# Expert weights kept as f16 parts in DRAM, expert products as three f16 products, and two arrays of expert sums

## The reference

```python
x = layernorm(x + attn(x))                    # x: 16 x 56 x 256, 16 heads of 16, rope, causal window
x = layernorm(x + xattn(x, ctx))              # ctx: 16 x 1500 x 256; q and out in int8 grids
x = layernorm(x + ffn(x))                     # 8 experts, top 2 of each token

gate_probs = softmax(x @ gate_w + gate_b)
weights, selected = top_k(gate_probs, 2);  weights /= weights.sum(-1)
comb = zeros((n, E)).at[arange(n)[:, None], selected].set(weights)
h = gelu(einsum('nd,edf->enf', x, w1) + b1[:, None, :])        # d = 256, f = 1024
expert_out = einsum('enf,efd->end', h, w2) + b2[:, None, :]
out = einsum('ne,end->nd', comb, expert_out)
```

## Time and profile before

| | us |
|---|---|
| median of 3 runs | 886.67 (882.23 to 886.75) |
| the profiled execution, its own time | 884.88 |
| its span | 883.1 |

### The profile page before, as it was taken

How to read it: one execution, slowest core, us unless ns; L and a number is a source line. 1 busy time by engine, 2 the same in 40 slices (tenths; PEclk the granted TensorE clock), 3 DMA queues, 4 the chain that set the end, 5 groups by cost and what they waited for, 6 DMA issues and landing times.

```text
span 883.1 us, 30182 instructions
## 1 busy us (share of the span) xinstructions
PE 800.3 (91%) x12379; PEld 608.1 (69%) x12379; DVE 632.6 (72%) x1234; ACT 511.2 (58%) x1084; POOL 260.6 (30%) x334
## 2 busy tenths in 40 slices
PE   5689998999999989999899999999997789999996
PEld 3356766666666666666676666767665569999995
DVE  5866776768777767776777778776864736588887
ACT  2336655666566546655665665656664443687782
POOL 4233223222612251225123421522240103133332
PEclk9999999999999999999999999999999789999999
DMA  7355544554555554554555555545466855766653
GB/s 220 108 149 160 159 137 133 152 164 131 160 148 147 160 149 128 163 152 143 148 151 156 153 158 158 172 136 160 138 190 177 294 195 182 215 202 184 205 155 95
DMA packets 91377, 143.25 MB, mean 162 GB/s; under 512 B 11423, under 2 KB 79583, under 8 KB 87918
## 3 DMA queue, kind: packets, MB, share of 16 engines
q1 hardware_dynamic: 87742, 136.74, 51.8%
q0 software_dynamic: 3504, 4.62, 2.7%
HBM read 101.60 MB, written 39.68 MB: 160 GB/s over the span
## 4 chain that ended last, share of the span: by engine, by line
PE 40%; DMA 29%; DVE 10%; SPq 7%; ACT 7%; issue 5%; DVEq 0%; POOLq 0%; POOL 0%; ACTq 0%
DMA k_dram<-k_two 15%; DMA sums<-y_sb,g_token 9%; PE ps L1613 8%; PE ps L1606 7%; PE ps L1687 5%; SPq L1079 5%; PE ps L1665 4%; DMA k_st<-k_dram 4%; ACT k_two L1368 3%; DVE k_two L507 3%; PE ps L1629 3%; PE ps L1923 3%; DVE negmax L513 2%; PE ps L1944 2%; PE ps L1697 2%
## 5 line engine op out<-in xcount | busy, mean ns | idle before, releaser
L513 DVE TENSOR_REDUCE negmax<-ps 112x1 f32<-112x1500 f32 x121 | 207.3, 1713 | 44.4 <-PE ps L1629 44.1
L1395 ACT ACTIVATE pT<-ps 125x448 f32<-125x448 f32 x384 | 195.8, 546 | 18.6 <-PE ps L1665 14.7
L1230 POOL TENSOR_TENSOR ctx_lo<-ctx_raw,ctx_hi 128x250 f16<-128x250 f32 x188 | 119.3, 666 | 229.7 <-DVE ctx_hi L498 212.8
L1665 PE MATMUL ps<-qbd,k_st 97*128 97x112 f16 x1536 | 129.4, 216 | 20.2 <-ACT qbd L1351 10.8
L1665 PEld LDWEIGHTS ps<-qbd,k_st 97*128 97x128 f16 x1536 | 92.9, 99 | 78.0 <-ACT qbd L1351 27.1
L507 DVE SCALAR_TENSOR_TENSOR k_two<-ps,bk_sb,k_two 128x500 f16<-128x500 f32 x96 | 70.7, 736 | 96.7 <-ACT k_two L1368 96.7
L1368 ACT ACTIVATE k_two<-ps,bk_sb 128x500 f16<-128x500 f32 x96 | 65.1, 678 | 91.6 <-PE ps L1606 68.6
L1351 ACT COPY v_sb<-ps 125x512 f32<-125x512 f32 x96 | 56.3, 587 | 89.5 <-PE ps L1613 89.4
L1687 PE MATMUL ps<-pT,v_sb 125*17 125x56 f32 x6144 | 93.4, 217 | 10.1 <-issue 10.1
L1687 PEld LDWEIGHTS ps<-pT,v_sb 125*17 125x17 f32 x6144 | 81.5, 100 | 29.5 <-issue 19.2
L1629 PE MATMUL ps<-k_st,qbd 96*112 96x500 f16 x363 | 97.4, 375 | 3.7 <-DMA k_st<-k_dram 2.9
(11 more groups left out here) (258 smaller groups left out, 1396.0 us busy)
## 6 DMA issues: line engine op xcount, KB each, us to landing
k_st<-k_dram SPq DMA_DIRECT2D x288, 125.0 KB, 2.6
w_sb<-w SPq DMA_DIRECT2D x25, 1024.0 KB, 5.1
ctx_raw<-ctx_T SPq DMA_DIRECT2D x48, 500.0 KB, 4.5
k_dram<-k_two SPq DMA_DIRECT2D x96, 250.0 KB, 3.6
xs<-zeros SPq DMA_DIRECT2D x28, 260.0 KB, 3.1
w_sb<-w SPq DMA_DIRECT2D x8, 512.0 KB, 4.9
xg<-xs SPq DMA_DIRECT2D x21, 130.0 KB, 4.1
a_x<-x_tok SPq DMA_DIRECT2D x8, 128.0 KB, 2.8
```

The source lines that it names most:

```text
L513: V.tensor_reduce(negmax[0:QW], ps[0:QW, BANK_S:BANK_S + CHUNKS, 0:MC], AX.XY, ALU.max, negate=True).then_inc(max_done, 1)
L1230: last = nc.gpsimd.tensor_tensor(ctx_lo[:, k, c2, a], ctx_raw[:, k, c2, a], ctx_hi[:, k, c2, a], ALU.subtract)
L1395: nc.scalar.activation(pT[0:MT, (PAIRS * b + p) % 3, TPC * g:TPC * g + TPC], ps[0:MT, BANK_T + n % 2, 0:TPC * QW].rearrange("p (t n) -> p ...
L1665: last = mm(ps[:, BANK_T + n % 2, QW * i:QW * i + QW], k_st[:, j, p, a:a + P], qbd[:, j, p].rearrange("p h s -> p (h s)"), start=True, sto ...
```

## The change

- GpSimd splits the weights of all experts once, in the first stage. There are 32 pieces of 128 x 1024 elements (`PIECES`): the w2 of experts 0 to 3, all w1, the w2 of experts 4 to 7. `split_piece` multiplies a piece by W_UP = 32 in place, copies it to f16, subtracts to get the low f16 part, and stores both parts in DRAM (`w1_parts`, `w2_parts`); then it issues the load of the piece after the next. All DMAs of a piece are issued by GpSimd. Its first operation waits for the store of the piece before. Five pieces go into each `iteration`: two, one and two (`split_pieces`), until the 32 are done in the seventh.
- Both expert products are three f16 products in all 21 tiles. `load_w1` reads the parts (again 1 MB per tile), `w2_sb` holds the parts of w2. VectorE makes `xgT_hi` and `xgT_lo` in place of `xgT`, and `h_lo` in all tiles; `w2_hi` and `w2_lo` are gone. The factor 32 is taken out in the gelu's scale and in the gate.
- There are two arrays of sums in DRAM, for even and odd tiles, so an add waits only for the one two tiles before. The odd array is cleared in the batches, read back at the end, and added by four more matmuls (`carried_odd`).
- In the early tiles the second product of a tile is placed behind the first product of the next, with the routing of the last token tile between them, and VectorE's order is changed to fit. SyncE clears the spare rows after it has issued the loads of w2, not ahead of them.

```diff
+        PIECES = [(2, e, i) for e in range(E // 2) for i in range(2)] + [(1, e, i) for e in range(E) for i in range(CH)] \
+            + [(2, e, i) for e in range(E // 2, E) for i in range(2)]
...
-                V.tensor_copy(xgT[:, g % 2], ps[:, XG_BANK, 0:D].rearrange("p (c n) -> p c n", c=CH)).then_inc(xgT_done, 1)
+                src = ps[:, XG_BANK, 0:D].rearrange("p (c n) -> p c n", c=CH)
+                V.tensor_copy(xgT_hi[:, g % 2], src).then_inc(xgT_done, 1)
+                dve.wait_ge(xgT_done, 2 * g + 1)
+                V.tensor_tensor(xgT_lo[:, g % 2], src, xgT_hi[:, g % 2], ALU.subtract).then_inc(xgT_done, 1)
...
-                if g > EARLY:
-                    dve.wait_ge(added, 16 * (g - 3))
+                if g >= 4:
+                    dve.wait_ge(added[g % 2], 16 * (g // 2 - 1))
...
             for g in range(EARLY, GT):
                 if g + 1 < GT:
                     xgT_step(g + 1)
-                w2_lo_step(g)
-                if g + 1 < GT:
                     gate(g + 1)
                 if g < GT - 1:
                     h_lo_step(g)
-                    if g > EARLY:
-                        y_step(g - 1)
+                    y_step(g - 1)
...
+            sp.wait_ge(w_parts_out, 16 * len(PIECES))
             for e in range(E // 2, E):
-                sp.dma_start(w2_sb[:, e], w2[e]).then_inc(w2_in, 16)
+                sp.dma_start(w2_sb[:, e], w2_parts[e].rearrange("i p n -> p i n")).then_inc(w2_in, 16)
...
+            def load_piece(n):
+                of, e, i = PIECES[n]
+                src = w1[e, :, i] if of == 1 else w2[e, :, 4 * i:4 * i + 4].rearrange("p f n -> p (f n)")
+                nc.gpsimd.dma_start(w_raw[:, n % 2], src).then_inc(raw_in[n % 2], 16)
...
+            def split_piece(n):
+                of, e, i = PIECES[n]
+                pool.wait_ge(raw_in[n % 2], 16 * (n // 2 + 1))
+                if n > 0:
+                    pool.wait_ge(w_parts_out, 16 * n)
+                raw = w_raw[:, n % 2]
+                nc.gpsimd.tensor_scalar(raw, raw, W_UP, None, ALU.mult).then_inc(w_parts_made, 1)
+                pool.wait_ge(w_parts_made, 3 * n + 1)
+                nc.gpsimd.tensor_copy(w_hl[:, 0], raw).then_inc(w_parts_made, 1)
+                pool.wait_ge(w_parts_made, 3 * n + 2)
+                nc.gpsimd.tensor_tensor(w_hl[:, 1], raw, w_hl[:, 0], ALU.subtract).then_inc(w_parts_made, 1)
+                pool.wait_ge(w_parts_made, 3 * n + 3)
+                nc.gpsimd.dma_start((w1_parts if of == 1 else w2_parts)[e, i],
+                                    w_hl[:].rearrange("p i n -> p (i n)")).then_inc(w_parts_out, 16)
+                if n + 2 < len(PIECES):
+                    load_piece(n + 2)
...
                 ctx_lo_step(2 * it + 1, 1, 2)
+                split_pieces(it, 0, 2)
                 ctx_lo_step(2 * it + 2, 0, 0)
                 if t_before is not None:
                     b_rstd_step(t_before)
                 ctx_lo_step(2 * it + 2, 0, 1)
+                split_pieces(it, 2, 3)
                 rstd_step(it + 1)
                 ctx_lo_step(2 * it + 2, 0, 2)
+                split_pieces(it, 3, 5)
                 qbd_step(it + 1, 0, 0)
...
-                if g > 0:
-                    pool.wait_ge(added, 16 * g)
+                if g > 1:
+                    pool.wait_ge(added[g % 2], 16 * (g // 2))
...
                     f = 4 * i + q
-                    for c in range(CH):
-                        last = mm(ps[:, H_BANK + 2 * par + i, P * q:P * q + P],
-                                  w1_sb[:, par, c, P * f:P * f + P], xgT[:, par, c],
-                                  start=(c == 0), stop=(c == CH - 1))
+                    for n, (x, w) in enumerate(SPLIT):
+                        for c in range(CH):
+                            last = mm(ps[:, H_BANK + 2 * par + i, P * q:P * q + P],
+                                      w1_sb[:, par, c, F * w + P * f:F * w + P * f + P], (xgT_hi, xgT_lo)[x][:, par, c],
+                                      start=(n == 0 and c == 0), stop=(n == 2 and c == CH - 1))
...
+                pe.wait_ge(h_lo_done, g + 1)
                 for f in range(FT):
                     if g == GT - 1 and f == 4:
...
+                        pe.wait_ge(h_lo_done, g + 2)
+                    for n, (x, w) in enumerate(SPLIT):
+                        a = F * w + D * (f % 4)
+                        last = mm(ps[:, Y_BANKS[g % 2], 0:D], (h_hi, h_lo)[x][:, par, f],
...
             for g in range(EARLY, GT):
                 m1_half(g, 0)
                 if g + 1 < GT:
                     tx(g + 1)
                 m1_half(g, 1)
-                if g > EARLY:
-                    m2_split(g - 1)
-            m2_split(GT - 1)
+                m2(g - 1)
+            for q in (2, 3):
+                carried_odd(q)
+            m2(GT - 1)
```

More of the change, by code:

```diff
@@ L360, in decoder_layer @@
         row_made = sem("row_made")
-        w2_hi_done = sem("w2_hi_done")
-        w2_lo_done = sem("w2_lo_done")
+        raw_in = [sem(f"raw_in{k}") for k in range(2)]
+        w_parts_made = sem("w_parts_made")
+        w_parts_out = sem("w_parts_out")
+        odd_in = sem("odd_in")
         h_hi_done = sem("h_hi_done")
@@ L376, in decoder_layer @@
         b2_in = sem("b2_in")
-        added = sem("added")
+        added = [sem(f"added{k}") for k in range(2)]
         gate_step = sem("gate_step")
@@ L1146, in _ @@
                 keys(B - 1, 1, u)
-                for e, f in ahead[:pieces]:
-                    sp.dma_start(w2_sb[:, e, f:f + half], w2[e, :, f:f + half]).then_inc(w2_ahead, 16)
+                sp.wait_ge(w_parts_out, 16 * E)
+                for e, i in ahead[:pieces]:
+                    sp.dma_start(w2_sb[:, e, i], w2_parts[e, i]).then_inc(w2_in, 16)
                 ahead = ahead[pieces:]
@@ L1262, in qbd_step, with split_pieces @@
                     pmask[:].unsqueeze(1).unsqueeze(3).to_broadcast([KS, 4, 2, S]), ALU.mult).then_inc(qbd_done, 1)
+            def load_piece(n):
[18 more added lines that the diff above has]
+                    load_piece(n + 2)
+            def split_pieces(it, first, last):
+                for n in range(5 * it + first, min(5 * it + last, len(PIECES))):
+                    split_piece(n)
             ctx_lo_step(0, 0, 1, True)
```

182 lines of the change are left out of this document (86 added, 96 removed).

## The result

The changed kernel takes 958.41 us (median of 4 runs, 952.15 to 962.83), the kernel before in the same comparison 884.7: ratio 1.084, interval 1.079 to 1.088. I had said 888, within 866 to 910. The profiled execution took 961.3 us, its span is 959.5. Medians are of all executions of a kernel, ratios only of those within 1.5% of its fastest (the fast state). Stages are read from the one profiled execution of each kernel, and the four executions of the changed kernel lie up to 11 us apart, so a difference of a few us between the batches of two kernels is not a finding.

What follows compares the result with a forecast made beforehand. TensorE was taken to bound both the batches and the expert stage. From 884.9 us: minus 20 for expert products, plus 18 for late qbd, plus 5 for port and DMA, 887.9, left at 888; range 866 to 910.

Steps and rivals of the forecast that it cites:

- What bounds the kernel: Batches and expert stage: TensorE bounds both, busy 298 of 320 us and all of 86; GpSimd has most room.
- 10.8 us of slack: SyncE's chain of keys in the batches: 10.8 us per pair spent waiting for keys to be made, taken as slack.
- Port and DMA: Batches: shared-port blocking and slower key landings from the pieces' traffic, 0.7 us x 7 = 5 us, bounds 0 and 20.
- Rival (c): Batches: SyncE's chain of keys becomes the bound, or pieces take 9 us and more; 910 us, chance 0.22.
- Its point of decision: SyncE's chain of keys in the batches: it becomes the bound from 0.8 us more per landing on.
- The sign that I had named for (c): Batches: SyncE no longer waits for keys to be made, if its chain of keys is the bound.
- Pieces on GpSimd: Batches: 32 pieces of 7.7 us each, bounds 6 and 11; two in a row 18.5 us, making qbd late.
- the term was 18: Batches: late qbd idles TensorE 4.3 us, less 1.3 of small waits; 3.0 us x 6 = 18 us lost.
- Expert products: Expert stage: f16 products save 27.7 us of TensorE time, 20 us after 7 off; bounds 14 and 25.
- rival (d): Expert products: weight loads don't keep up, 128-column matmuls take 84 ns instead of 56; 915 us, chance 0.07.
- lie under that wait: End of kernel: the added odd read and four f32 matmuls are hidden while TensorE waits for sums read back.
- Two arrays: Late expert loop: one chain of adds, 6.5 us each, would bind at 5.5 us tiles; two keep the 20 us.

Runs made afterwards that it cites:

- free chain: Changed kernel with 4 of 32 pieces, SyncE loading keys from a constant place without waiting for their store's landing: 849.8 us, ratio 0.962.
- transfers-only kernel: Changed kernel with all loads and stores of the 32 pieces, without their three operations and the wait for the store before: 950.4 us, ratio 1.075.
- SyncE's places: Changed kernel with all piece transfers and no arithmetic, issued by SyncE where it waits for keys to be made, not by GpSimd: 931.6 us, ratio 1.052.
- the first place: Changed kernel with only 14 pieces, two behind the last ctx_lo of chunk 2 in each of seven pairs of batches: 906.6 us, ratio 1.024.
- the delays without traffic: Kernel before, with a waited-for 64-byte transfer and an unwaited one in SyncE's queue ahead of unit 6's keys, in 14 batches: 927.5 us, ratio 1.046.
- unit 11: Kernel before, with a waited-for 64-byte transfer and an unwaited one in SyncE's queue ahead of unit 11's keys, in 14 batches: 906.5 us, ratio 1.012.
- transfers alone with the free chain: Changed kernel with all piece transfers, no arithmetic, and SyncE loading keys from a constant place without waiting for their store's landing: 881.9 us, ratio 0.995.

## Why the prediction was wrong, by its steps

**What bounds the kernel.** "Both stages are TensorE's" was the first error. TensorE busy for 298 of 320 us hides that the batches' pace hangs on two things at once. The free chain shows it: 28 us gained with the number of TensorE's matmuls unchanged. The chain of waits on the page had it, and I had weighed it only as 10.8 us of slack.

**Port and DMA: the step that failed.** I had put 5 us for slower keys, with 20 as the upper bound. By transpose 0, the transfers alone make 77.9 us (794.06 in the transfers-only kernel against 716.2), and all the rest of the pieces 6.8 (800.90; by the ratios 8). 77.9 over 32 pieces is 2.4 us for a piece's 1.05 MB. I had multiplied a slower landing by the few places where TensorE already waits, and had used the mean landing. The median landing did rise by only 0.5 us (3.6 to 4.1), as I had thought; what decides is that a key stored behind a piece and a chunk lands late, after 4.9 to 8.8 us instead of 3.2, and there are ten transfers per pair, which lasts 98 us now (between the first pieces of two pairs) where I had 87 to 89. The Trainium skill (DMA: Bandwidth & Descriptors, Anatomy of one DMA) fits a transfer by 2.0 us and its bytes over 436 GB/s, and (same page, Queues, rings and completion order) says that each engine takes turns between the queues a packet at a time. By the first, the bytes of a piece take 2.4 us, an estimate. The runs' 2.4 us per piece is the same number, but not the same quantity: it is idle time and a lower clock, and it was 1.9 us per piece in SyncE's places, 2.8 in the first place and 1.1 with the free chain. So the agreement is no proof. The turns agree with keys that are stored behind a piece and land late.

A second term I had at nothing: TensorE's clock. 31.2 of the 84.7 us are its busy time at a granted clock of 0.94 instead of 0.98. I had priced each wait at its length. That waits alone do this is shown by the delays without traffic, where 12.7 of 34.8 us are busy time.

Rival (c) had the right place, the keys' chain, with a chance of 0.22 and the wrong size, 27 us instead of 78. Its point of decision, 0.8 us more per landing, came from the same wrong slack: the slack was never used up. The sign that I had named for (c), SyncE no longer waiting for keys to be made, did not appear; from 100 to 700 us it waits 93.2 us for them, before 76.9. Delays of 4.2 us at unit 6 cost 2.9 each, so it decides from about 1 us per batch there.

**Pieces on GpSimd.** A piece takes 7.6 us and I had 7.7. Its parts were off in both directions: the multiplication in place 2.77 us (I took 1.1), the copy 1.1, the subtraction 2.2 (2.4), the two issues with their gap 1.5 instead of 2.9. The groups of the page:

```profile
L1288 POOL TENSOR_SCALAR w_raw<-w_raw 128x1024 f32<-128x1024 f32 x32 | 88.7, 2772 | 60.3 <-DMA w_parts<-w_hl 60.3
...
L1292 POOL TENSOR_TENSOR w_hl<-w_raw,w_hl 128x1024 f16<-128x1024 f32 x32 | 71.4, 2230 | 2.7
```

The wait for the store before is 4.3 us as a mean (60.3 over 14), where I had 3.0; two pieces in a row take 17.6 to 21.4 us, within my 14 to 25. `qbd` is then late as said (TensorE's waits, 60 to 760 us):

```profile
PE ps L1663 <- POOL qbd L1269: 21.4, 6, 4.2
```

3.6 us each, six times; I had 4.3. So the part on which most of my working went was right (21.4 us of wait, the term was 18), and on top of the transfers it is worth only 7 of the 85 us. That when keys and `qbd` are late together only the later one counts would explain this; it was not tested by itself.

**Expert products.** TensorE as forecast: first product 2.68 us, second 2.62, a late tile 5.6 us where I had 5.5. That is rival (d) refuted: 56 ns per matmul of 128 columns with its weights. By the figure of the Trainium skill (TensorE: Matmul & The Clock Gate, Back-to-back issue gap), 81 ns, the first product would be 3.9 us, an estimate; the trace disagrees. But the stage as a whole gained 8.2 us where I had 20, under my lower bound of 14: 14.7 in the late loop, and the gains around the loop are missing. In the early stage I had 2 to 3 us, and 0.1 came: TensorE waits 1.0 to 1.5 us ahead of each first product, since the second product that used to stand between a transpose and its use has moved behind it. The five waits (tiles 1 to 5) sum to 6.1 us, and I had not listed the move. Of the odd read and its matmuls I had said that they "lie under that wait", and the end lost 6.6 us: a wait of 3.33 us for 1 MB in front of the last second product, and matmuls at the lower clock level behind it.

**Two arrays.** That one chain of adds would bind at 5.5 us per tile was wrong. With one array an add is issued, lands and is followed by the next within 4.7 us (its median landing is 4.5 us, where the kernel before has 5.6), so the 6.5 us that I had put together from the earlier trace rows were too much, and the second array bought nothing for its read at the end.

## What to carry to other kernels

Ahead of adding traffic to a stage, look on the page at which transfers are in the chain that ended last: if one of them is waited for in line, don't price added traffic by the share of idle DMA engines, which were idle nearly half of the time here and a megabyte still cost 1.9 to 2.8 us with the wait in line, 1.1 with most of it gone. Price a stall of TensorE above its length, since the granted clock fell after stalls too: here a good third of the batches' loss (31.2 of 84.7 us) was slower matmuls. Measure slack by putting a pure delay at the place, since waits added up over a stage say nothing about where they lie. And when a step's order is changed, list what used to cover each result's way to its user; a product moved away from between a transpose and its use cost what the faster product gained.

## What the runs showed of the hardware

- A 64-byte DRAM-to-DRAM transfer issued by SyncE took 3.2 us (median, delays at unit 6; 3.5 at unit 11) from issue to landing, hardly less than 250 KB of keys in the kernel before (3.6).
- GpSimd multiplied 128 x 1024 f32 elements by a constant in place in 2.77 us and copied them to f16 in 1.09 (changed kernel): the one-input operations differ by a factor of 2.5, and the multiplication is slower than the two-input subtraction (2.23).
- A plain transfer of 512 KB cost GpSimd 0.54 to 0.88 us per issue (loads, median 0.55), its indirect stores of rows 1.0.
- TensorE stood still for 4.53 us between two matmuls of one line, with nothing in the profile to wait for; four transfers of 512 KB had been issued from 253.1 to 255.4 us, the stall began near 258.8 (transfers alone with the free chain).
- A pure delay in SyncE's queue, without traffic, lowered TensorE's mean granted clock up to transpose 0 from 0.98 to 0.96.
